# Both attentions: the sums of values of a head in two half-width parts

## What is computed

```python
# first attention: scores with two relative terms, clipped to +-64
scores = einsum('bhqd,bhkd->bhqk', Q, K) * scale
scores = scores + c2p + swapaxes(p2c, -1, -2)      # gathered by relative position
probs = softmax(scores, axis=-1)
ctx = einsum('bhqk,bhkd->bhqd', probs, V)
# second attention: scores with sinusoid positions, shifted
scores = (term1 + term3 + _rel_shift(term2 + term4)) / sqrt(dk)
attn = softmax(scores, axis=-1)
out = einsum('bhqk,bhkd->bqhd', attn, V)
```

## Time and profile before

| | us |
|---|---|
| three runs: median (lowest, highest) | 2112.28 (2108.89, 2114.2) |
| the profiled execution | 2112.18 |
| its span, first to last instruction | 2110.4 |
| busy in the span: PE | 1724.6 |
| busy: DVE | 1468.4 |
| busy: ACT | 1466.8 |
| L644, sums of values, 2048 records | 272.4, 606 ns each |
| L830, copies of a group's sums | 64 (32 in each attention) |

### The profile page before, as it was taken

One profiled execution on the slowest core, in us unless ns is written; L12 is line 12 of the kernel. 1 busy time (PEld: TensorE's weight loads), 2 busy tenths in 40 slices (PEclk: granted clock), 3 DMA queues, 4 the chain that ended last, 5 costly groups with the idle time before them and its releaser, 6 DMA issues. The chain is left out here.

```text
span 2110.4 us, 44034 instructions
## 1 busy us (share of the span) xinstructions
PE 1724.6 (82%) x11670; PEld 1044.7 (50%) x11670; DVE 1468.4 (70%) x3508; ACT 1466.8 (70%) x2584; POOL 79.4 (4%) x102
## 2 busy tenths in 40 slices
PE   2316999999999999983861799999999994999998
PEld 1203555555555555552540465565556552545544
DVE  2635888888888888872983788888888882423422
ACT  2304888888888888881872799999999993223222
POOL 0000000000000000000540000000000000000000
PEclk9656999999999999996985899999999997999999
DMA  2966999998899999955687777777777763100100
GB/s 71 353 217 195 271 270 276 275 269 271 271 274 277 270 271 276 272 163 153 206 299 257 200 210 213 213 213 211 212 212 213 211 180 100 35 20 22 37 5 10
DMA packets 419996, 420.89 MB, mean 199 GB/s; under 512 B 36016, under 2 KB 325320, under 8 KB 419808
## 3 DMA queue, kind: packets, MB, share of 16 engines
q1 hardware_dynamic: 419936, 420.19, 67.1%
HBM read 232.47 MB, written 187.00 MB: 199 GB/s over the span
## 5 line engine op out<-in xcount | busy, mean ns | idle before, releaser
L817 ACT ACTIVATE a_prob<-bank,a_negmax 128x512 f32<-128x512 f32 x1024 | 734.6, 717 | 51.3 <-DVE a_negmax L749 49.6
L749 DVE TENSOR_REDUCE a_negmax<-bank 128x1 f32<-128x512 f32 x1024 | 699.5, 683 | 0.2 <-issue 0.2
L631 PE MATMUL bank<-a_ident,a_prob 128*128 128x128 f32 x4096 | 644.1, 280 | 60.1 <-ACT a_probt L824 50.8
L824 ACT COPY a_probt<-bank 128x512 f32<-128x512 f32 x1024 | 616.2, 602 | 87.4 <-PE bank L631 73.7
L631 PEld LDWEIGHTS bank<-a_ident,a_prob 128*128 128x128 f32 x4096 | 449.5, 141 | 181.9 <-issue 76.5
L741 DVE TENSOR_TENSOR bank<-bank,a_band 128x128 f32<-128x128 f32 (+3 forms) x1024 | 350.2, 342 | 80.1 <-PE bank L612 68.4
L610 PE MATMUL bank<-a_stks 65*128 65x192 bf16 (+7 forms) x1024 | 323.0, 316 | 10.5 <-ACT a_prob L817 10.2
L644 PE MATMUL bank<-a_probt,a_vs 128*32 128x512 f32 x2048 | 272.4, 606 | 15.0 <-ACT a_probt L824 15.0
L610 PEld LDWEIGHTS bank<-a_stks 65*128 65x128 bf16 (+1 forms) x1024 | 100.1, 98 | 231.8 <-ACT a_prob L817 202.4
L729 DVE COPY_PREDICATED bank<-a_mask,bank 128x128 f32<-128x128 uint32 (+1 forms) x512 | 139.4, 272 | 107.2 <-PE bank L616 107.1
L612 PE MATMUL bank<-a_stks 65*128 65x320 bf16 (+5 forms) x768 | 201.1, 262 | 0.0
(11 more groups left out here) (169 smaller groups left out, 1567.9 us busy)
## 6 DMA issues: line engine op xcount, KB each, us to landing
a_band<-shear_b SPq DMA_DIRECT2D x128, 512.0 KB, 4.4
shear_a<-a_keyside SPq DMA_DIRECT2D x128, 256.0 KB, 3.4
a_sheared<-shear_a SPq DMA_DIRECT2D x128, 256.0 KB, 4.4
shear_b<-a_corr SPq DMA_DIRECT2D x128, 256.0 KB, 4.4
shear_e<-a_corr SPq DMA_DIRECT2D x128, 256.0 KB, 2.3
a_band<-shear_e SPq DMA_DIRECT2D x128, 256.0 KB, 3.4
a_stks<-stack SPq DMA_DIRECT2D x128, 192.0 KB, 4.5
a_stks<-stack SPq DMA_DIRECT2D x128, 144.0 KB, 2.9
```

The lines of the kernel that those rows point to most:

```text
L631: last = pe.transpose(turned_bank[k][:, n * 128:(n + 1) * 128], prob[h.slot % 2][:, n, k * 128:(k + 1) * 128], ident[:, :])
L749: v.tensor_reduce(negmax[h.slot % 2][:, n:n + 1], score[:, :], AX.X, ALU.max, negate=True).then_inc(maxed, 1)
L817: nc.scalar.activation(prob[h.slot % 2][:, n, :], score[:, :], ACT.Exp, bias=negmax[h.slot % 2][:, n:n + 1]).then_inc(exped, 1)
L824: nc.scalar.copy(probt[h.slot][:, k, :], turned_bank[k][:, :]).then_inc(copied, 1)
```

## The change

`weigh` gets a parameter `half`. The first key block of a group (k = 0) stays one sum of full width and is made at the first turn of step 0. The other three blocks are made in two parts: columns 0 to 255 after the first turn of their step, columns 256 to 511 after the third turn. Only the second parts (and the whole k = 0 block) count on `pv_mm`, so the group's total stays 16. `group_out` on ACT moves from behind the second turned copy of the group's last step to behind the fourth.

```diff
-                    def weigh(pe, h, k):
+                    def weigh(pe, h, k, half):
...
                         if k == 0:
                             pe.wait_ge(v_in[g], BASE + 16 * (h.i + 1))
                             pe.wait_ge(out_copied, BASE + h.use(GROUP))
                             pe.wait_ge(copied, BASE + 4 * (h.n + GROUP))
+                        q = slice(0, T) if k == 0 else slice(half * T // 2, half * T // 2 + T // 2)
                         for j in range(GROUP):
                             at = VC * (NT * j + k)
-                            pe.matmul(cbank[32 * j:32 * j + VW, :], vs[g][:, at:at + VW], probt[h.slot + j][:, k, :],
-                                      start=(k == 0), stop=(k == NT - 1)).then_inc(pv_mm, 1)
+                            part = pe.matmul(cbank[32 * j:32 * j + VW, q], vs[g][:, at:at + VW], probt[h.slot + j][:, k, q],
+                                             start=(k == 0), stop=(k == NT - 1 and half == 1))
+                            if k == 0 or half == 1:
+                                part.then_inc(pv_mm, 1)
...
                             turn(pe, own, k)
-                            if k == 0 and weighed:
-                                weigh(pe, Head(i, j - j % GROUP - GROUP), j % GROUP)
+                            if weighed and (k == 0 or k == 2 and j % GROUP > 0):
+                                weigh(pe, Head(i, j - j % GROUP - GROUP), j % GROUP, k // 2)
...
                         for k in range(NT):
-                            weigh(pe, Head(loops, FIRST + last - GROUP), k)
+                            for half in range(2 if k else 1):
+                                weigh(pe, Head(loops, FIRST + last - GROUP), k, half)
...
                                 copy_turned(act, own, k)
-                                if k == 1 and weighed and j % GROUP == GROUP - 1:
+                                if k == 3 and weighed and j % GROUP == GROUP - 1:
                                     group_out(act, Head(i, j - j % GROUP - GROUP))
```

## The result

The changed kernel takes 2219.4 us (median of four runs, 2197.3 to 2224.9) against 2113.2 us: a ratio of 1.0487, 95% interval 1.0411 to 1.0563. The direction was forecast, the size was not: +106 us where +24 was expected, and outside the range that ended at 2166.

A forecast was written before the change was run, and what follows sets the result against it. First attention bound by a one-head ring over PE, DVE and ACT, the second by ACT. Per group -3 x 0.42 + 3 x 0.05 + 1.9 = +0.79 us, times 30 = +24 us: 2136 us, range 2097 to 2166.

The forecast's parts named there:

- The ring: First attention: a one-head loop over PE, DVE and ACT, 5.97 us, with the sum's whole 1.00 us on it.
- part 1: First attention, three of four heads: sums in halves of 0.57 us make each such head 0.42 us shorter.
- a later band: First attention, halved heads: the shorter period leaves the band read less time, costing 0.05 us a head (0 to 0.2).
- The 0.1 us for missing increments: First-half matmuls carry no semaphore increment; four fewer would save another 0.1 us in three heads of four; left out.
- Part 3: Group's copy moved behind the fourth turn's: SP's waiting store delays the next band read, costing 1.9 us per group.
- bounds of the delay: First attention's ring delay per group from the late band read: 1.1 us (landing 3.5) to 3.3 us (landing 5.5).
- Part 4: Second attention: ACT is the bound, so halves and moved copy change 0, bounds -5 and +10 us over the phase.
- the halves win: Rival, chance 0.17: first attention's late read costs nothing worth naming, -1.11 us per group, 2079 us in all.

The follow-up runs named there:

- copy_late_only: The kernel before with only the group's copy moved behind the fourth turned copy, in both attentions, all sums at full width: 2219.8 us, ratio 1.0501.
- late_store: The changed kernel with the first attention's group store on SP behind the next head's band read and band write instead of ahead: 2116.7 us, ratio 1.0010.
- light_late_store: late_store with less DMA traffic in the first attention (parts of the scores left out); second attention halved in two steps of four, copy at its old place: 2082.5 us.

## Why the prediction was wrong, point by point

- **The missing term, the granted clock**: this is the step that failed. The prediction read 1.00 in the earlier trace rows, concluded that "durations there can be added", and priced everything at the upper level, also behind the stall that it forecast itself: its term for the clock is nothing. In the runs the clock fell 29 times in the first attention, each time with a stretch of 1.5 us or more in which PE did almost nothing in the 4 us ahead of it. The price is 53.8 us, two thirds of the 82 us by which the forecast was short.
- **The ring and part 1** (0.42 us a halved head): right in the mechanism. A half takes 0.57 us to the next matmul at a granted clock of 1.00, as worked out. With transfers out of the way DVE's wait ahead of the old L729 falls from 0.81 us (86.4 us, 107 times, 240 to 880 us) to 0.32 (44.1, 139 times), where 0.35 was forecast, and the halves give 34.0 us where 30 x 1.11 = 33 was forecast. That match is in part luck: the 1.11 has 0.15 us for a later band in it, which light traffic does not have, and without it 31 x 1.26 = 39 us. With the band late and the clock kept up they give 28.7. The 0.1 us for missing increments, kept out of the sum, is not seen between matmuls: in the second attention a first half without increments (1599.76) and a second half with four (1602.04) both take 0.57 us to the next matmul.
- **Part 3 on SP**, the named mechanism: right, and alone enough for the whole slowdown (`copy_late_only`). The term was too small: 792.5 - 719.9 = 72.6 us where 30 x 1.9 = 57 stood, 2.3 us a group. A wait of 2.45 us was forecast; the long ones are 2.7 us in the mean, and single ones reach 4.2 us, where the upper bound (a landing of 5.5 us and the full 2.56) allowed 3.9. The prediction's own bounds of the delay, 1.1 to 3.3 us, give 2112 to 2178 by its sum; the 2119 to 2155 and the end at 2166 were narrower than that without a reason given. The measured 2219 lies outside all of them.
- **Part 4, the second attention**: the copy costs nothing, as said; the halves cost 11.7 us where the upper bound was 10. The prediction compared busy sums (17.3 against 17.99 us) and did not ask who waits for the turn that the second half pushes back.
- **The rival "the halves win"**: `late_store` took the store out of the band read's way, and the halves still did not win, since landings become the bound at once. The prediction had priced that at 0.05 us a head; `late_store` shows 717.9 - 683.4 = 34.5 us, 0.37 us in each halved head. In the changed kernel little of it shows (25 waits for the band, nearly all long ones behind a store); by my reading, not shown, the stall gives the queue time.

The sum by runs: late band +72.6, halves -28.7, clock +53.8: +97.7 us in the first attention; +11.7 in the second; 3.3 us of the span are elsewhere. The forecast had +57, -33, 0 and 0. The first three are steps from one phase length to the next (719.9, 792.5, 763.8, 817.6), so they add up by construction and their sum confirms nothing. The split leans on the repeats, which also add work and leave 10 to 20 us at the lower clock, and on single profiled executions, so each term may be off by several us. No version tried that computes the whole is faster than the kernel before.

## What to carry to other kernels

A copy that is free on its own engine may be what another queue waits for: before moving it, list what stands behind the waiting instruction. Here that one move cost some 106 us (2219.8 against 2114.1). When a forecast contains a stall of PE, price the matmuls behind it at the lower clock as well. And when one bound is taken away, look for the next at the same height: here the ring over PE and a bound that goes with the band's landings both gave some 720 us.

## What the runs showed of the hardware

- PE busy 0.08 and 0.17 us in two slices of one us was followed by a granted clock of 0.50 for about 3.5 us, then 1.00. Over the first attention the changed kernel spent 184 us at the lower level in 29 falls; with repeats of a matmul in the gap it was 10 us. Adding eight matmuls a group made the kernel 54 us faster (2219.4 to 2165.3).
- Landing times depend on more than the mean share of the DMA engines: a 256 KB band read (512 KB moved as the page counts it) took 3.7 us in the median at a share of 0.77 (light_late_store), 4.4 at 0.91 (the kernel before) and 5.2 at 0.92 (late_store). Between the last two the order of issues and the pace of the heads differ, not the share.
- Four fp32 sums onto 32 partitions each, 256 instead of 512 columns wide, take 0.57 instead of 1.00 us to the next matmul at a granted clock of 1.00, and 1.02 us at 0.50.
